# Attention and expert kernel: a hand-ordered head, a new order of the steady steps, weight splits three a step

## The reference

```python
x = x + attn(layernorm(x), w_qkv, w_out)
#  q, k = elu(rope(q) * S) + 1, elu(rope(k) * S) + 1
#  kv += k_t v_t ; ks += k_t ; out_t = q_t kv / max(q_t ks, 1e-6)   (per head, over the tokens)
x = x + ffn(layernorm(x), Wg, Wu, Wd, Wr, temperature)
#  w = routing weights of sigmoid(x Wr / T): a zone test, else the two nearest experts
#  out = sum_e w_e * (silu(x Wg_e) * (x Wu_e)) Wd_e,   8 experts of width 256, all of them computed
```

## Time and profile before

| | |
|---|---|
| median of 3 runs | 891.44 us (890.34 to 892.09) |
| the profiled execution, its own time | 891.97 us |
| its span, first to last instruction | 890.0 us |
| first `gate` matmul (end of the head) | 114.87 us |
| busy: TensorE, VectorE, ScalarE, GpSimd | 799.0, 690.3, 487.8, 528.1 us |
| mean granted TensorE clock | 0.946 of full |

### The profile page before, as it was taken

How to read it: one execution, slowest core, us unless ns; L and a number is a source line. 1 busy time by engine, 2 the same in 40 slices (tenths; PEclk the granted TensorE clock), 3 DMA queues, 4 the chain that set the end, 5 groups by cost and what they waited for, 6 DMA issues and landing times.

```text
span 890.0 us, 18338 instructions
## 1 busy us (share of the span) xinstructions
PE 799.0 (90%) x6792; PEld 666.7 (75%) x6792; DVE 690.3 (78%) x1562; ACT 487.8 (55%) x902; POOL 528.1 (59%) x577
## 2 busy tenths in 40 slices
PE   3355588899999998999999998999899998999997
PEld 2244467678778887888788887888788887888886
DVE  5455668788988898888988888889988898875433
ACT  2444465666566664666566664666566665654221
POOL 2466667776566665666566665666466665663332
PEclk7555579999999999999999999999999999999999
DMA  3333322322311122121211102211311210120000
GB/s 103 80 67 78 83 46 63 95 49 39 61 27 25 23 39 60 37 36 39 60 38 32 26 21 58 37 37 39 60 37 37 33 29 26 24 25 1 24 1 24
DMA packets 97305, 38.29 MB, mean 43 GB/s; under 512 B 74176, under 2 KB 96960, under 8 KB 97216
## 3 DMA queue, kind: packets, MB, share of 16 engines
q1 hardware_dynamic: 90688, 30.83, 17.1%
q10 hardware_dynamic: 6528, 6.29, 2.4%
HBM read 16.13 MB, written 4.19 MB: 23 GB/s over the span
## 4 chain that ended last, share of the span: by engine, by line
PE 59%; DVE 17%; POOL 9%; issue 7%; ACT 6%; DMA 2%; SPq 1%; ACTq 0%; DVEq 0%; POOLq 0%
PE y L419 14%; PE gate L386 13%; PE up L386 13%; PE front L267 5%; POOL a_lo L1079 3%; PE front L268 2%; DVE xa L975 2%; PE back L312 2%; DVE work L963 2%; PE front L377 2%; PE back L290 2%; DVE rop L730 2%; DMA kT<-k_st 1%; PE back L323 1%; ACT L601 1%
## 5 line engine op out<-in xcount | busy, mean ns | idle before, releaser
L1107 POOL TENSOR_TENSOR h_lo<-work,h_hi 128x512 fp32r<-128x512 f32 x128 | 165.7, 1294 | 122.3 <-ACT h_hi L608 122.2
L1079 POOL TENSOR_TENSOR a_lo<-am,a_hi 128x512 f16<-128x512 f32 x120 | 137.5, 1166 | 47.9 <-ACT a_hi L543 47.8
L419 PE MATMUL y<-wd_hi,h_hi 128*128 128x256 f32 x512 | 151.2, 295 | 1.6 <-DVE xa L975 1.1
L419 PE MATMUL y<-wd_lo,h_hi 128*128 128x256 f32 x512 | 142.9, 279 | 0.0
L419 PE MATMUL y<-wd_hi,h_lo 128*128 128x256 f32 x512 | 142.8, 279 | 0.0
L963 DVE TENSOR_TENSOR work<-work,up 128x512 f32<-128x512 f32 x128 | 87.2, 682 | 46.4 <-PE up L386 36.9
L975 DVE SCALAR_TENSOR_TENSOR xa<-y,wo,xa 128x256 f32<-128x256 f32 x256 | 108.4, 474 | 8.7 <-PE y L419 8.7
L543 ACT ACTIVATE a_hi<-am 128x512 f16<-128x512 f32 x120 | 75.3, 629 | 72.5 <-DVE am L754 71.6
L608 ACT ACTIVATE h_hi<-work 128x512 fp32r<-128x512 f32 x128 | 80.0, 625 | 47.0 <-PE y L419 38.5
L419 PEld LDWEIGHTS y<-wd_hi,h_hi 128*128 128x128 f32 x512 | 96.2, 188 | 4.1 <-DVE xa L975 1.7
L419 PEld LDWEIGHTS y<-wd_lo,h_hi 128*128 128x128 f32 x512 | 96.4, 188 | 0.7
(11 more groups left out here) (184 smaller groups left out, 1882.0 us busy)
## 6 DMA issues: line engine op xcount, KB each, us to landing
xr<-xT SPq DMA_DIRECT2D x32, 128.0 KB, 2.5
xa<-x SPq DMA_DIRECT2D x32, 128.0 KB, 2.8
out<-xa SPq DMA_DIRECT2D x32, 128.0 KB, 1.8
xa<-Wg ACTq DMA_DIRECT2D x8, 256.0 KB, 2.7
work<-Wu ACTq DMA_DIRECT2D x8, 256.0 KB, 2.7
work<-Wd ACTq DMA_DIRECT2D x8, 256.0 KB, 3.1
work<-w_qkv SPq DMA_DIRECT2D x1, 768.0 KB, 5.1
qT<-q_st SPq DMA_TRANSPOSE x32, 3.2
```

The source lines that it names most:

```text
L419: m = pe.matmul(Y[t // 2][:, t % 2 * D:(t % 2 + 1) * D], h_p[hi][:, n % 2, t * P:(t + 1) * P], wd_p[wi][:, u // KI, u % KI, :], start=(n % ...
L1079: pool.tensor_tensor(a_p[1][:, heads(r), :], am_place(g, r).rearrange("p (h n) -> p h n", h=4), a_p[0][:, heads(r), :], ALU.subtract).then ...
L1107: pool.tensor_tensor(h_p[1][:, n % 2, :], hb[:, n % 2, :], h_p[0][:, n % 2, :].bitcast(F32), ALU.subtract).then_inc(s_hlo, 1)
```

## The change

In words: (1) the head is no longer a loop, but 5 lists of calls, in which tiles overlap (`qkv(1)` comes ahead of `scores(0, 0)`); (2) the scores of tiles 0 to 3 use G and Y1 only, two halves one after the other; (3) each of the four engines' steady loops has a new order, TensorE's with `av`, `state`, `o_T` and `proj` further apart and `x2_T` next to `scores`; (4) slabs go three a step in the first eight steps, 15 in the head and 9 in three steady steps, and in the head every third `slab_lo` (2, 5, 8, 11, 14) is VectorE's, with a semaphore of its own; (5) two one-column `idle` memsets get a column each; SyncE's loads are wrapped in functions in the same order. No arithmetic is added or removed.

```diff
-            return (R2, R3, G, Y1)[r] if g < NT else BK[r % 2]
+            return (G, Y1)[r % 2] if g < NT else BK[r % 2]
...
-            n = 2 * s + i if s < LAG else 2 * LAG + 5 * (s - LAG) + i
-            return n if i < (2 if s < LAG else 5) and n < SLABS else None
+            n = 3 * s + i
+            return n if i < 3 and n < SLABS else None
...
-            return s_slab_lo, n + 1
+            if n < 3 * LAG and n % 3 == 2:
+                return s_slab_lov, n // 3 + 1
+            return s_slab_lo, n + 1 - min(n // 3, LAG)
...
-                if g < NT and half:
+                if half:
+                    w.wait_ge(s_amask, 4 * g + 2)
+                elif g < NT:
                     w.wait_ge(s_amask, 4 * g)
-                elif half:
-                    w.wait_ge(s_amask, 4 * g + 2)
...
-            for s in range(LAG):
-                a, c, d = s, s - 1, s - 2
-                scores(c, 0); scores(c, 1); qkv(a); x2_T(d); av(c); state(c); logit(d); o_T(c); proj(c)
-            scores(LAG - 1, 0); x2_T(LAG - 2); logit(LAG - 2); scores(LAG - 1, 1)
+            qkv(0); qkv(1); scores(0, 0); scores(0, 1); qkv(2); av(0); state(0); scores(1, 0); scores(1, 1); o_T(0)
+            proj(0); qkv(3); av(1); x2_T(0); state(1); scores(2, 0); o_T(1); scores(2, 1); proj(1); logit(0); qkv(4)
+            av(2); x2_T(1); o_T(2); state(2); proj(2); scores(3, 0); scores(3, 1); logit(1); x2_T(2); av(3)
+            logit(2); o_T(3); state(3); proj(3); scores(4, 0); x2_T(3); scores(4, 1); logit(3)
             for s in range(LAG, STEPS):
...
-                gate(n); qkv(a); up(n); av(c); down(n - 2)
-                gate(n + 1); up(n + 1); o_T(c); down(n - 1)
-                gate(n + 2); state(c); up(n + 2); proj(c); down(n)
-                gate(n + 3); scores(a, 0); up(n + 3); x2_T(c); down(n + 1); scores(a, 1)
+                gate(n); qkv(a); up(n); down(n - 2); av(c); gate(n + 1); down(n - 1); state(c); up(n + 1); o_T(c)
+                gate(n + 2); proj(c); up(n + 2); gate(n + 3); down(n); x2_T(c); scores(a, 0); up(n + 3); down(n + 1)
+                scores(a, 1)
...
-                a_hi(c, 2); a_hi(c, 3); silu(n); slab_hi(slab(s, 0)); qk_copy(a); v_copy(a); v1(a)
-                exp(a); e1(router); fb(router); h_hi(n); q_hi(a); k_hi(a); silu(n + 1); v2(a)
-                slab_hi(slab(s, 1)); slab_hi(slab(s, 2))
-                o_hi(c); h_hi(n + 1); x_hi(a + 1); silu(n + 2); s1(c)
-                s2(c); h_hi(n + 2); slab_hi(slab(s, 3)); silu(n + 3); a_hi(a, 0); x2_hi(c); a_hi(a, 1)
-                slab_hi(slab(s, 4))
+                a_hi(c, 2); silu(n); a_hi(c, 3); qk_copy(a); h_hi(n - 1); e1(router); fb(router)
+                slab_hi(slab(s, 0)); exp(a); silu(n + 1); q_hi(a); k_hi(a); v_copy(a); o_hi(c); h_hi(n); h_hi(n + 1)
+                v1(a); silu(n + 2); slab_hi(slab(s, 1)); s1(c); silu(n + 3); s2(c); h_hi(n + 2); x2_hi(c)
+                x_hi(a + 1); a_hi(a, 0); slab_hi(slab(s, 2)); a_hi(a, 1); v2(a)
...
+            def slab_lo(n):
+                if n is None or slab_lo_done(n)[0] is not s_slab_lov:
+                    return
+                _, dst, e_ = slabs[n]
+                w.wait_ge(s_slab_hi, n + 1)
+                v.tensor_tensor(dst[1][:, e_, :, :], ring[n % NSL], dst[0][:, e_, :, :].bitcast(F32),
+                                ALU.subtract).then_inc(s_slab_lov, 1)
...
+            tcos_scale(0); wout_lo(); x_lo(1); cos(0); rope(0); phi(0); tcos_scale(1); q_lo(0); x_lo(2); cos(1)
+            rope(1); tcos_scale(2); slab_lo(2); mask(0, 0); phi(1); mask(0, 1); mask(0, 2); mask(0, 3); q_lo(1)
+            cos(2); o_sum(0, 0); o_sum(0, 1); den_max(0); st_add(0); den_rec(0); norm(0); x_lo(3); mask(1, 0)
...
+            o_sum(3, 0); mean_var(5); o_sum(3, 1); den_max(3); den_rec(3); norm(3); slab_lo(11); var_eps(5); o_lo(3)
+            x_lo(5); st_add(3); x1_add(3); bn2(3); mean_var2(3); var_eps2(3); mask(4, 0); ln2(3); mask(4, 1)
+            x2_lo(3); slab_lo(14)
             for s in range(LAG, STEPS):
...
-                acc(n - 4, 0); acc(n - 4, 1); mask(c, 2); mask(c, 3); acc(n - 4, 2); acc(n - 4, 3)
-                route_zone(router); tcos_scale(a); route_nearest(router); cos(a); h_up(n); o_sum(c, 0); rope(a)
-                o_sum(c, 1); den_max(c); route_weight(router); den_rec(c); phi(a); norm(c); q_lo(a); h_up(n + 1)
-                route_first(router); o_lo(c); route_second(router); acc(n - 2, 0); acc(n - 2, 1); route_tie(router)
-                acc(n - 2, 2); acc(n - 2, 3); route_ix2(router); st_add(c); x_lo(a + 1); route_s2(router); bn(a + 1)
-                mean_var(a + 1); route_sum(router); h_up(n + 2); var_eps(a + 1)
-                x1_add(c); bn2(c); mean_var2(c); var_eps2(c); route_out(router)
-                ln2(c); mask(a, 0); mask(a, 1); h_up(n + 3); x2_lo(c)
+                mask(c, 2); tcos_scale(a); acc(n - 4, 0); acc(n - 4, 1); mask(c, 3); bn(a + 1); acc(n - 4, 2)
+                route_zone(router); route_nearest(router); acc(n - 4, 3); cos(a); mean_var(a + 1); h_up(n)
+                route_weight(router); rope(a); o_sum(c, 0); o_sum(c, 1); den_max(c); route_first(router); den_rec(c)
+                phi(a); norm(c); route_second(router); q_lo(a); o_lo(c); h_up(n + 1); st_add(c); var_eps(a + 1)
+                route_tie(router); acc(n - 2, 0); x1_add(c); bn2(c); mean_var2(c); var_eps2(c); acc(n - 2, 1)
+                route_ix2(router); acc(n - 2, 2); acc(n - 2, 3); ln2(c); h_up(n + 2); mask(a, 0); route_s2(router)
+                x2_lo(c); mask(a, 1); h_up(n + 3); route_sum(router); route_out(router); x_lo(a + 1)
...
+            slab_lo(0); sin(0, 1); sin(0, 0); v_rest(0); k_lo(0); sin(1, 1); sin(1, 0); slab_lo(1); v3(0)
+            a_lo(0, 0); k_lo(1); a_lo(0, 1); a_lo(0, 2); a_lo(0, 3); sin(2, 1); slab_lo(3); v_rest(1); slab_lo(4)
...
+            v3(3); slab_lo(9); sin(4, 0); slab_lo(10); rstd2_pow(2); st_rest(2); a_lo(3, 0); a_lo(3, 1); a_lo(3, 2)
+            s3(2); a_lo(3, 3); k_lo(4); v_rest(4); rstd1_pow(5); slab_lo(12); slab_lo(13); rstd2_pow(3); a_lo(4, 0)
+            st_rest(3); a_lo(4, 1); s3(3); v3(4)
             for s in range(LAG, STEPS):
...
-                h_lo(n - 1); a_lo(c, 2); a_lo(c, 3); sin(a, 1); sin(a, 0); slab_lo(slab(s, 0))
-                v_rest(a); h_lo(n); k_lo(a); v3(a); slab_lo(slab(s, 1)); slab_lo(slab(s, 2))
-                h_lo(n + 1); rstd1_pow(a + 1); st_rest(c); s3(c)
-                rstd2_pow(c); h_lo(n + 2); slab_lo(slab(s, 3)); a_lo(a, 0); a_lo(a, 1); slab_lo(slab(s, 4))
+                a_lo(c, 2); a_lo(c, 3); sin(a, 1); sin(a, 0); h_lo(n - 1); slab_lo(slab(s, 0)); k_lo(a); h_lo(n)
+                h_lo(n + 1); rstd1_pow(a + 1); rstd2_pow(c); st_rest(c); v_rest(a); slab_lo(slab(s, 1)); h_lo(n + 2)
+                a_lo(a, 0); a_lo(a, 1); v3(a); s3(c); slab_lo(slab(s, 2))
```

80 lines of the change are left out of this document (36 added, 44 removed).

## The result

| | before | after |
|---|---|---|
| median of 4 runs | 891.06 us (890.34 to 892.09) | 858.57 us (858.27 to 859.25) |
| ratio, 95% interval | | 0.9636 [0.9619, 0.9652] |
| span of the profiled execution | 890.0 us | 856.6 us |
| first `gate` matmul | 114.87 us | 97.06 us |
| mean granted TensorE clock | 0.946 | 0.964 |

The account below looks back on a forecast made before the run. TensorE, busy 799.0 of 890.0 us, sets most of the span, with VectorE the bound in routing steps. Head -15.5, first three steps -8.5, routing -16.5, plain +4 sum to -36.5: 855 us by the median, range 840 to 876.

Parts of the forecast that it names:

- Head: Start to first gate: overlapping tiles shorten it by 15.5 us, to about 99.5; bounds 5 and 24.
- 15.8 us a tile for the pair: Head: VectorE and GpSimd, excluding each other, need 15.8 us a tile; with lists not filled wholly, 17 taken.
- A split on VectorE: Head: a weight split moved to VectorE still shuts GpSimd out and adds 0.69 us a tile to the pair.
- Two banks: Head: two score banks for four cost some 1.3 us of mask waits per tile, beside GpSimd's work.
- First three steps: First three steady steps: 14 splits become 9, 84.56 becomes 76.0, -8.5 us; bounds -3 and -11.
- Routing steps: Six routing steps: fewer VectorE and GpSimd collisions, 27.44 to 24.7 us each, -16.5 us; above 26 would be wrong.
- `rope`: Routing steps: waiting for sin, it will find GpSimd busy and take 1.70 us instead of 0.72, +1.0.
- collisions only change places: Rival for the routing steps: they stay at 27.4 us, total 872 us; chance 0.15.
- -2.95: 27.44 becomes 24.5: Routing steps: sum of VectorE's collision gains and losses, taken off the step; 24.7 with a little idle.
- Plain steps: The 18 other steps of the 24: 0.2 us added to each, +4 us; bounds 0 and +14.
- two tight places: Plain steps: gate(n+3) 0.1 us late; ln2 ends at 18.7 or 19.5, x2_T wants it at 19.3.
- The slower case: Rival in the steady steps: silu(n + 1) behind exp(a) on ScalarE comes late, 904 us; chance 0.05.

Follow-up runs that it names:

- e1_head_only: New head, split schedule and two score banks of the changed kernel, steady loops in the order of the kernel before: 873.48 us, 0.9797 of before.
- e5_pool_splits: Changed kernel with VectorE's five weight splits of the head back on GpSimd: 858.66 us, 0.9630 of the kernel before.
- e6_two_banks: Kernel before with the scores of tiles 0 to 3 in two banks instead of four: 897.67 us, 1.0068 of before.
- e9_splits_apart: New head with old steady orders, the third split of a step moved away from the second: 869.87 us, 0.9760 of the kernel before.
- e2_steady_only: Kernel before (its head, banks and split schedule) with the four new steady orders, splits four and five at the step's end: 885.69 us, 0.9934.
- e4_route_early: Changed kernel with route_tie, route_ix2, route_s2 ahead of q_lo, route_sum ahead of mask(a, 0), x_lo ahead of route_out: 840.53 us, 0.9428 of before.
- e8_s2_later: Changed kernel with early routing, but route_s2 just ahead of mask(a, 0) and route_sum at the step's end: 840.39 us, 0.9428 of before.
- e3_xlo_first: Changed kernel with x_lo(a + 1) ahead of route_sum and route_out on VectorE: 857.71 us, 0.9616 of the kernel before.
- e7_splits_last: New head with old steady orders, second and third split moved to the end of the step: 874.06 us, 0.9803 of the kernel before.

## Why the prediction was right, and where it was not

The time: 855.0 us was forecast with 840 to 876, and it is 858.57; faster, as expected with 0.93. Against each profiled execution's own time, -36.5 was forecast and -33.3 came (891.97 to 858.69). That the sum is so near is in good part luck. In the spans the routing steps with the ones behind them fell short by 13.9 us (-2.6 for -16.5), and the head (2.3), the first three steps (3.2) and the twelve other steps (4.9, -0.9 for +4) made up 10.4 of it. By its steps:

- **Head, -15.5 forecast, -17.8 measured.** That the new head alone brings this is shown by e1_head_only, and the chain's links (`kT`, `k_hi`, `a_lo`) are shorter as forecast; which of its moves does it stays open. The parts were off in both directions. Periods of 17 were forecast for the three landings after tile 0; they are 13.99, 13.39 and 17.69, 15.0 on average, and give 13.9 us where 8 were summed. The term that was mis-sized is "15.8 us a tile for the pair": VectorE and GpSimd as a floor, which two of the three periods are below. It took GpSimd's busy time of one period of before, with whatever GpSimd lost there to VectorE in it, and gave each tile an equal share of work that a list can put elsewhere. In the third period the two were busy for 16.34 and 15.28 of 17.69 us; in the first two for 9.58 and 11.49 of 13.99, and 11.23 and 10.64 of 13.39, so they carry less. How much each of the two reasons weighs was not separated. The end, from tile 3's `kT` to `gate`, gave 3.7 and not 6.5, the start 0.2 and not 1.
- **A split on VectorE.** The forecast counted 0.69 us a tile for it against the pair. By the rows a split would hold the pair for 0.69 us on VectorE and for 1.29 on GpSimd, and e5_pool_splits finds no difference (858.66 for 858.57), so the pair's time, counted like this, is not what sets the head's length. By the Trainium skill (SBUF - State Buffer, Who interferes with whom) such a split shuts GpSimd out for its length; that run doesn't contradict it and doesn't show it.
- **Two banks.** "A wait of two masks per tile, some 1.3 us": 1.6 us a tile in e6_two_banks. The size was near. In the old order it lay on the chain; whether it "lies beside GpSimd's work" in the new one no run shows, and `scores` do wait for the masks there (6.9 us in 4).
- **First three steps, -8.5 forecast, -11.7 measured.** That is just outside the bounds of -3 and -11. The reason given, five splits fewer, does not carry it alone: with the splits fewer and the old lists it is -0.9 (e1_head_only), so the reason was half of it. Missing in the working was that a load's issue stands in ScalarE's stream and waits there for a buffer, so where the splits stand counts (4.3 us, e9_splits_apart), and that the first routing step is long in the old order (30.38, 30.93 in e1_head_only, 29.67 in e9_splits_apart) and not in the new (24.29 in e2_steady_only, 24.50 in after).
- **Routing steps, -16.5 forecast, -7.6 measured, and +5.0 in the steps behind them.** This is the step that failed: 26.26 us is above the 26 that the prediction itself named as a sign of being wrong. The meetings that it followed came as forecast or better, but for `rope`, whose +1.0 did not come in these steps. It did not follow the rest of the routing instructions that move: the one of 1.26 us and "the first two of the routing behind one `a_lo` and not two" were costed, and `route_tie`, `route_s2` and `route_out` were taken at their 0.2 us of before. They went to 1.22, 1.12, 1.10 and 0.80. The rival of this case, "collisions only change places", named the mechanism and took it as whole. With the steps behind counted, it was 13.9 of 16.5 us, so the rival was nearer here than the forecast. The forecast also summed VectorE's time as the bound ("-2.95: 27.44 becomes 24.5"). VectorE's busy time did fall by 3.56, from 25.87 to 22.31, but part of that is calls that now run in the next step; over the two steps it fell by 2.85 (45.96 to 43.11), as forecast, and the two together got shorter by 0.37 us only. With 4 us idle VectorE was no longer a bound, and what counted was which three waits of TensorE stood behind a held instruction. e4_route_early shows it: VectorE busy for 21.08 and the step at TensorE's own 23.75.
- **Plain steps, +4 forecast, +5.0 - 0.9 measured.** Right in sum by chance, wrong in place: neither of the two tight places that the hand count found (`gate(n + 3)`, `x2_T`) costs anything, 23.75 us being TensorE's pace. All of it lies in the six steps behind a routing step, on `x_lo` and so on the routing. `x_lo` was costed at nothing, since "VectorE has 3.7 us idle in a plain step". That was the wrong cover: the call stands at the end of a routing step, where there was none.
- **The slower case** (`silu(n + 1)` behind `exp`) did not come: no wait of `gate` on `silu` is among the step's.

## What to carry to other kernels

Where two engines hold each other up, an instruction's duration belongs to its place and not to its shape: in a new order, write down for every small instruction that moves, not just for the large ones, what the other engine does at that time, and who on the critical engine stands behind it. An engine's busy time tells what a step is worth only while that engine is full; once it has idle time, count the waits of the critical engine one by one and put the small independent work where the other engine is known to wait. Ahead of a DMA issue that waits for a buffer, look at the compute calls behind it in the same stream.

## What the runs showed of the hardware

In the timelines above, VectorE instructions of 0.18 us take up to 1.2 us when they start within one of GpSimd's, and end within 0.05 us of the end of that one. This also holds for one that reads a single SBUF tile of 128 x 4: L960, 0.17 us before and 0.80 here, from 416.80 to 417.60, with GpSimd's `a_lo` ending at 417.57. By the Trainium skill (SBUF - State Buffer, Who interferes with whom) whichever of the two starts first holds the port pair for its whole instruction, and the ends of L929, L942 and L944 agree. Not every VectorE instruction is held: L883, a reduction of 128 x 32, starts at 393.48 within an `a_lo` (393.37 to 394.58) and takes 0.19 us.

The same code of the head gives first `gate` between 97.06 and 98.86 us from one profiled execution to another, and the granted clock between 57 and 76 us goes with it loosely. Kernel after (columns as in the windows above):

```profile
57.00:76.00 19.00, 11.95 (x134) 9.94 (x130) 16.94 (x38) 10.05 (x23) 16.59 (x19) 0.79 0.49 101
```

and e4_route_early, whose head is the same:

```profile
57.00:76.00 19.00, 12.43 (x144) 9.85 (x142) 17.38 (x38) 9.08 (x22) 15.12 (x17) 0.67 0.47 94
```

With the clock at 0.79 the first `gate` comes at 97.06, with 0.67 at 98.86; e9_splits_apart (0.79, 97.06), e1_head_only (0.81, 97.51), e8_s2_later (0.65, 98.01) and e3_xlo_first (0.66, 98.84), all with the same head, go the same way; e7_splits_last (0.69, 97.28) doesn't, so the clock of this stretch isn't the whole of it. These shares lie between TensorE's two levels, 1.2 and 2.4 GHz. TensorE's busy share of the stretch is 63% in after and 65% in e4_route_early, so the trace doesn't show why one execution is granted the higher level for more of it than the other. A difference of under 2 us between two single profiled executions of such a head can't be put down to an edit.
